# A graph network's build stage: its comparisons take their ramps from PSUM, and its products are evicted in halves from three PSUM regions

## The reference, cut to what matters

```python
x = _layernorm(x + _L0_gnn_ref(x, ..., src, dst, edge_type_3, node_type_3))   # typed messages, summed per node
x = _layernorm(x + _L1_gnn_ref(x, ..., edge_index, edge_weight))              # weighted sum of support[col] per row
x = _layernorm(x + _L2_gnn_ref(edge_index, x))                                # degree-normalised sum of neighbours
x = _layernorm(x + _L3_gnn_ref(x, edge_attr_64, src, dst, ...))               # sum of edge features @ W and h[src]
```

## Time and profile before

| | us |
|---|---|
| median of 3 runs (5166.46 to 5170.2) | 5168.8 |
| the profiled execution | 5166.42 |
| its span in the profile | 5164.6 |

### The profile page before, as it was taken

How to read it: one execution, slowest core, us unless ns; L and a number is a source line. 1 busy time by engine, 2 the same in 40 slices (tenths; PEclk the granted TensorE clock), 3 DMA queues, 4 the chain that set the end, 5 groups by cost and what they waited for, 6 DMA issues and landing times. The chain is left out here.

```text
span 5164.6 us, 99803 instructions
## 1 busy us (share of the span) xinstructions
PE 3645.9 (71%) x38930; PEld 2640.2 (51%) x38930; DVE 3255.0 (63%) x4527; ACT 1201.7 (23%) x2110; POOL 2201.7 (43%) x2050
## 2 busy tenths in 40 slices
PE   4457755555555555102888887399999599989997
PEld 3345655555555555102777776255555244444444
DVE  7886899999999999202777775766666500230022
ACT  0015655555555555100000000300000200010000
POOL 0051277777777777775777775000000003000300
PEclk9998899999999999656999999699999799989998
DMA  9646799999999999758878777288886367656664
GB/s 315 222 106 226 259 316 334 349 347 344 354 342 345 352 348 345 266 157 156 230 228 229 228 230 181 92 320 305 301 308 250 121 202 228 200 164 201 218 190 138
DMA packets 710790, 1297.10 MB, mean 251 GB/s; under 512 B 367384, under 2 KB 512428, under 8 KB 701260
## 3 DMA queue, kind: packets, MB, share of 16 engines
q1 hardware_dynamic: 579516, 823.86, 49.2%
q10 hardware_dynamic: 60300, 314.88, 15.5%
q0 software_dynamic: 70576, 152.66, 11.7%
HBM read 814.90 MB, written 529.03 MB: 260 GB/s over the span
## 5 line engine op out<-in xcount | busy, mean ns | idle before, releaser
L1394 POOL DMA_INDIRECT big<-typed_msgs,big x1216 | 1374.6, 1130 | 402.4 <-issue 365.7
L1439 PE MATMUL psum<-big 128*128 128x98 bf16 x7936 | 844.9, 206 | 607.3 <-DVE big L1421 567.7
L1439 PEld LDWEIGHTS psum<-big 128*128 128x128 bf16 x7936 | 761.3, 96 | 659.7 <-DVE big L1421 615.1
L2081 PE MATMUL psum<-big 128*128 128x512 bf16 (+1 forms) x4704 | 992.4, 374 | 82.5 <-DMA big<-adj 82.5
L1440 PE MATMUL psum<-big 128*128 128x49 bf16 x7936 | 831.4, 189 | 0.1
L1441 PE MATMUL psum<-big 128*128 128x49 bf16 x7936 | 829.0, 185 | 1.6 <-issue 1.6
L1441 PEld LDWEIGHTS psum<-big 128*128 128x128 bf16 x7936 | 782.0, 99 | 2.2 <-issue 2.1
L2081 PEld LDWEIGHTS psum<-big 128*128 128x128 bf16 x4704 | 460.4, 98 | 606.0 <-DMA big<-adj 83.0
L1440 PEld LDWEIGHTS psum<-big 128*128 128x128 bf16 x7936 | 765.6, 96 | 0.8 <-issue 0.7
L1666 PE MATMUL psum<-big 128*128 128x192 f32 x3648 | 643.8, 331 | 124.1 <-DMA big<-typed_msgs,big 105.1
L1891 PE MATMUL psum<-big 128*128 128x416 f32 x1984 | 656.4, 494 | 63.5 <-DVE big L1925 62.4
(11 more groups left out here) (318 smaller groups left out, 2799.0 us busy)
## 6 DMA issues: line engine op xcount, KB each, us to landing
wadj<-big ACTq DMA_DIRECT2D x248, 784.0 KB
big<-wadj SPq DMA_DIRECT2D x124, 1568.0 KB, 7.0
big<-adj SPq DMA_DIRECT2D x210, 896.0 KB, 4.8
big<-staged SPq DMA_DIRECT2D x304, 384.0 KB, 4.1
staged<-big SPq DMA_DIRECT2D x60, 1920.0 KB
adj<-big ACTq DMA_DIRECT2D x62, 1568.0 KB
big<-edge_feats SPq DMA_DIRECT2D x456, 128.0 KB, 4.2
edge_feats<-in_edge_attr SPq DMA_DIRECT2D x1, 51562.5 KB, 161.6
```

The costliest lines, as they stand in the source:

```text
L1394: pool.indirect_dma_start(out=sgot4[:, c, u, 0:D], out_offset=None, in_=typed_rows, in_offset=bass.IndirectOffsetOnAxis(ap=pairs4i[:, g, u ...
L1439: pe.matmul(to[:, 0:2 * NB], lo, hi_b[:, q, t, 0:2, 0:NB], start=True, stop=False)
L2081: last = pe.matmul(ps[c % 2][:, 0:len(blocks) * P], terms_[:, k, b * D:(b + 1) * D], ring_a[:, m % RA, 0:len(blocks), s * P:(s + 1) * P], ...
```

## The change

- Two groups of PSUM words, at the ends of banks 6 and 7, receive a copy of both ramps (89 words each). L1416 and L1418 read the ramp from there: blocks with even number from bank 6, with odd number from bank 7. The values compared with them and the three weight terms of L1421 stay in SBUF. (`term_words` is defined and not used.)
- The products go to three regions of two banks, each for eight nodes, where there were two regions of four banks for sixteen. PE counts `s_mm_b` per half batch and waits with half m until half m - 3 is evicted. DVE's and POOL's waits on `s_mm_b` are doubled in number and mean the same batches.
- ACT evicts each half by two copies of 8 x 49 = 392 elements; stores, loads and doubling stay where they were, after the second half. As the region is m mod 3, ACT's loop over the pairs of blocks is unrolled.

```diff
+        def made_in(q):
+            return psum[:, q * 1024:(q + 1) * 1024].rearrange("p (k x) -> p k x", k=2)[:, :, 0:4 * 2 * NB].rearrange("p k (t c) -> p k t c", c=2 * NB)
+        REGIONS, HALF = 3, TT // 2
+        def ramp_words(k):
+            return psum[:, (7 + k) * 512 - RAMP_WORDS:(7 + k) * 512]
+        def psum_ramps(k):
+            both = ramp_words(k).bitcast(BF16)
+            return both[:, 0:P], both[:, P:P + HC]
...
-                            at_least(pool, s_mm_b, i * (2 * BATCHES) + c * (2 * BATCHES) // SPER - BEHIND)
+                            at_least(pool, s_mm_b, 2 * (i * (2 * BATCHES) + c * (2 * BATCHES) // SPER - BEHIND))
...
+                for k in range(2):
+                    dve.tensor_copy(ramp_words(k), both_ramps).then_inc(s_clear, 1)
...
-                            dve.tensor_tensor(hi, in_twos(hi_ramp).to_broadcast([P, TT, HC // 2, 2]), all_columns(sbk, HC),
+                            dve.tensor_tensor(hi, in_twos(psum_ramps(k)[1]).to_broadcast([P, TT, HC // 2, 2]), all_columns(sbk, HC),
                                               ALU.is_equal).then_inc(s_hi_b, 1)
                             dve.tensor_tensor(lo_b[:, q, :, :].rearrange("p t (c d) -> p t c d", d=2),
-                                              in_twos(lo_ramp).to_broadcast([P, TT, P // 2, 2]), all_columns(sl, P), ALU.is_equal)
+                                              in_twos(psum_ramps(k)[0]).to_broadcast([P, TT, P // 2, 2]), all_columns(sl, P), ALU.is_equal)
...
-                        at_least(pe, s_adj_e, n - 1)
+                    at_least(pe, s_adj_e, m + 1 - REGIONS)
+                    for j in range(HALF):
+                        t = half * HALF + j
+                        to = made_in(m % REGIONS)[:, j // 4, j % 4, :]
...
+                            for half in range(2):
+                                m = 2 * (i * (2 * BATCHES) + k * BATCHES + b) + half
+                                act.wait_ge(s_mm_b, m + 1)
+                                made = made_in(m % REGIONS)
+                                t0 = b * TT + half * HALF
+                                act.copy(adj_st[:, k, :, t0:t0 + HALF].rearrange("p s (c t) -> p s c t", c=2),
+                                         made[:, :, :, 0:NB].rearrange("p c t s -> p s c t"))
+                                act.copy(wadj_st[:, k, b // 2, :, t0 % 32:t0 % 32 + HALF].rearrange("p s (c t) -> p s c t", c=2),
+                                         made[:, :, :, NB:2 * NB].rearrange("p c t s -> p s c t")).then_inc(s_adj_e, 1)
...
-                block_pairs(act, body)
+                for i in range(GB // 2):
+                    body(i)
```

More of the change, by code:

```diff
@@ L1239, in build @@
         hi_b = c.bitcast(BF16).rearrange("p (k t s c) -> p k t s c", k=2, s=4, c=HC)
-        c, at = cut(at, (P + HC + 1) // 2)
-        c = c.bitcast(BF16)
+        both_ramps, at = cut(at, (P + HC) // 2)
+        c = both_ramps.bitcast(BF16)
         lo_ramp, hi_ramp = c[:, 0:P], c[:, P:P + HC]
@@ L1348, in made_in, with term_words @@
         def made_in(q):
-            return psum[:, q * 2048:(q + 1) * 2048].rearrange("p (t c) -> p t c", c=P)
+            return psum[:, q * 1024:(q + 1) * 1024].rearrange("p (k x) -> p k x", k=2)[:, :, 0:4 * 2 * NB].rearrange("p k (t c) -> p k t c", c=2 * NB)
+        REGIONS, HALF = 3, TT // 2
+        RAMP_WORDS, TERM_WORDS = (P + HC) // 2, 3 * SLOTS
+        assert HC % 2 == 0 and RAMP_WORDS + TERM_WORDS <= 512
+        def ramp_words(k):
[3 more added lines that the diff above has]
+            return both[:, 0:P], both[:, P:P + HC]
+        def term_words(k):
+            return psum[:, (6 + k) * 512:(6 + k) * 512 + TERM_WORDS]
         with nc.Block() as block:
@@ L1404, in _ @@
                 dve.wait_ge(s_clear, 3)
+                for k in range(2):
+                    dve.tensor_copy(ramp_words(k), both_ramps).then_inc(s_clear, 1)
+                dve.wait_ge(s_clear, 5)
                 def body(i):
@@ L1428, in _, with half_batch @@
             def _(pe):
[L1429 to L1433, removed]
+                pe.wait_ge(s_clear, 5)
+                def half_batch(n, half):
+                    q, m = n % 2, 2 * n + half
+                    if half == 0:
                         pe.wait_ge(s_hot_b, n + 1)
-                        at_least(pe, s_adj_e, n - 1)
[L1436 to L1444, removed]
+                    at_least(pe, s_adj_e, m + 1 - REGIONS)
+                    for j in range(HALF):
+                        t = half * HALF + j
+                        to = made_in(m % REGIONS)[:, j // 4, j % 4, :]
+                        lo = lo_b[:, q, t, :]
+                        pe.matmul(to[:, 0:2 * NB], lo, hi_b[:, q, t, 0:2, 0:NB], start=True, stop=False)
+                        pe.matmul(to[:, NB:2 * NB], lo, hi_b[:, q, t, 2, 0:NB], start=False, stop=False)
+                        last = pe.matmul(to[:, NB:2 * NB], lo, hi_b[:, q, t, 3, 0:NB], start=False, stop=True)
+                    last.then_inc(s_mm_b, 1)
+                for n in range(NBATCH):
+                    for half in range(2):
+                        half_batch(n, half)
             @block.scalar
@@ L1456, in store @@
                     if b == 0:
-                        act.wait_ge(s_adj_e, i * (2 * BATCHES) + (k + 1) * BATCHES)
+                        act.wait_ge(s_adj_e, 2 * (i * (2 * BATCHES) + (k + 1) * BATCHES))
                     if b in WADJ_AT:
@@ L1582, in _ @@
                 dve.memset(psum[:, 0:Q * 512], 0.0).then_inc(s_clear, 1)
-                dve.wait_ge(s_clear, 5)
+                dve.wait_ge(s_clear, 7)
                 def one_hot(i, pos):
@@ L1645, in _ @@
             def _(pe):
-                pe.wait_ge(s_clear, 5)
+                pe.wait_ge(s_clear, 7)
                 def turn(i, own_):
```

2 lines of the change are left out of this document (1 added, 1 removed).

## The result

| | us |
|---|---|
| before, median of 14 runs (5160.61 to 5175.1) | 5168.45 |
| changed, median of 14 runs (5151.86 to 5161.56) | 5158.43 |
| ratio, with its 95% interval | 0.9981 (0.9973 to 0.9989) |
| the changed kernel's profiled execution, its span | 5155.02, 5153.2 |

The change gains 10 us of 5168, 0.19%. That is clear of the noise, since the interval of the ratio ends at 0.9989, and within the 0.2% that were called no change. In the changed kernel the gather of the staging is L1411, the two comparisons are L1436 and L1438, the product L1441, ACT's copies L1505 and L1507.

The account below looks back on a forecast made before the run. The prediction took POOL's row of gathers, locked in step with DVE's batches, to bound the build stage. 5166.4 + 0 (freed port) + 2 (comparisons) + 0 (halves, regions) = 5168 us; range 5140 to 5228.

Parts of the forecast that it names:

- the 0.2% that were called no change: Whole kernel: under 0.2% (10 us) a measurement can't tell from no change; chance of landing there 0.62.
- What bounds the stage: Build stage: POOL's row of gathers ends it; DVE, PE and ACT have 285 us of cover.
- Freed port, 0 us: Ramps from PSUM: comparisons stop delaying gathers, but the wait moves into the product, still two gathers per batch; 0 us.
- Rival (a): Gathers in the build: no lock, the comparison's 0.38 us per batch vanishes; -188 us, 4978 us; chance 0.07.
- The price of the comparisons, +2 us: DVE's two comparisons reading PSUM: -4 to +10 us over 496 batches, taken as +2.
- Rival (b): DVE's comparisons fall to the single pace, 1.50 us more per batch; +449 to +452 us, 5616 us; chance 0.12.
- The 65 ns more per instruction: DVE's PSUM reads: cycle table puts the fixed part 62 cycles above SBUF's, which would make the sum +64 us.
- Halves and three regions, 0 on the path: PE and ACT: split copies cost ACT 147 us, covered by its slack; 0 us, ends -27 and +51.
- rival (c): Thinner PE/ACT buffers: block-start waits reach DVE, over 30 us idle; +30 to +51 us, 5205 us; chance 0.11.
- The range's low end: Whole kernel: 5166 - 4 - 27, given as rounded up to 5140 us.
- The end of -218 us for the freed port: Ramps from PSUM, best case: 0.45 us of gather waiting freed per batch, 218 us in all.

Follow-up runs that it names:

- the mirror image: Changed kernel with ramps in SBUF, weight terms read from PSUM: 5936.7 us, ratio 1.0039 to the kernel before; with a third of the matmuls 5669.0 us, 0.959.
- halves_only: Changed kernel with both ramps read from SBUF again, halves and unrolled ACT code kept: 5926.0 us, ratio 1.0011 to the kernel before.
- third_after: Changed kernel with one of PE's three matmuls per node: 5669.8 us, ratio 0.957 to the kernel before.
- longer_batch: Changed kernel plus a DVE memset of 192 PSUM words per batch, ahead of the product: 5820.4 us, ratio 0.9837 to the kernel before; repeated 5822.8, 0.9852.
- third_longer: longer_batch with a third of the matmuls: 5635.7 us, ratio 0.952 to the kernel before, without one execution of 5939.6 us.

## Why the prediction came out as it did

**What bounds the stage: right.** POOL is all but alone from 2120 us on; without PE's matmuls the time is the same; and once no gather waits, the stage is 136 us shorter with DVE's end where it was.

**Freed port, 0 us: right, and by its mechanism.** Gathers of 0.94 and 1.38 us in turn were forecast and measured to 0.01 us, and two gathers start in 467 of the 468 batches in which DVE isn't held up. The same rule forecast the pattern of the mirror image and the wait in the longer batch; it did not forecast the gathers that wait near the memset. Rival (a), that the freed waits pay, is out. One of the rows behind it was miscounted: from 2423.36 to 3187.02 us not 100 but 145 gathers start inside an L1613. Of these 144 take 0.93 to 0.95 us, and the one of 1.48 starts in the last 6 ns of its L1613 and inside an L1588, so the reading stands.

**The price of the comparisons, +2 us: small as forecast, with the other sign.** They keep the double pace: 1212 ns for 2048 elements against 1215, 567 for 800 as before. Rival (b) is out, and with it the single rate that the Trainium skill gives in "VectorE: DVE Perf Modes", § The perf-mode tier table, for a tensor_tensor with a PSUM operand, at least for bf16 ramps of this form; the condition in the Trainium skill's "Vector Engine (DVE) Microarchitecture Reference", § 5.1, which names no memory, agrees. The 65 ns more per instruction, worked out in the prediction from the Trainium skill's cycle table, don't show either. The mean distance from start to start, over the undisturbed batches of the build, fell from 2.940 to 2.932 us, and 496 x 0.008 = 4 us is nearly all by which the last gather moved (4.6 us). That it comes of the ramps' place, and not of the halves or of the changed waits, the batches of halves_only and third_after show. The rows of the forecast gave -4 to +10 us; the value taken was at the wrong side of zero.

**Halves and three regions, 0 on the path: right, but ACT's cost was too low.** The copies take 500 and 564 ns, not 480 and 510, so ACT is busy 1055 us with them instead of 839, 216 more rather than 147. The fixed part was taken from a copy of another shape; the order in which a copy reads its region changed too, and the two aren't told apart. ACT's waits for the store of adj rose from 117 to 175 us, DVE's waits for PE from 10.5 us at 11 places to 28.9 at 21. With 2.8 us more of "issue" that is 31.7 us of idle time, at the mark of 30 that was set for rival (c), and DVE's last comparison starts 18 us later (2117.2 for 2099.6). POOL's last gather came 4.6 us earlier nevertheless, so POOL's sum took nothing of it, as argued, and the price of rival (c), 30 to 51 us, is out.

**The rest.** Forecast 5168, measured 5158. Of the 11.4 us between the two spans 6.4 are there when the next block's first gather starts (2404.4 and 2398.0): 4.6 at the last gather and nearly 2 in the seam. The other 5 arise later, in code that is the same. Runs of one kernel differ by 10 to 15 us, so these 5 are left unexplained. That the total fell within the 0.2% is therefore in part luck: the sum has no term for more than half of the 10 us. The range's low end was rounded the wrong way, since its terms give 5135 and not 5140; nothing hangs on it.

**The end of -218 us for the freed port was too far out.** It ignored that the transfers of the build stood at 0.98. Where all waits were gone, 142 us came.

## What to carry to other kernels

When one engine's short steps wait for another's long ones, follow the starts through one period before counting freed waits as gains: the two lock, and what counts is how many steps end in a period, a whole number. Removing part of the blocking only moves the wait; here the first half gave nothing, the other half alone only changed the pattern, and with both the waiting was gone and the time fell by what the next limit, probably the transfers, left of it. Count over a whole trace, too, and not only in one stretch: it was the count that showed the gathers near the memset, for which a rule read from a few rows did not hold. A version with both from PSUM and all its matmuls never ran where it could win, so its 142 us are shown only for the kernel without matmuls.

## What was unexpected of the hardware

- Among these three operations a gather waits only for one with two SBUF inputs, not for one that reads PSUM and SBUF: all 1216 took 938 to 957 ns once each of the three had one input in PSUM. That is as the Trainium skill has it in "SBUF — State Buffer", § Who interferes with whom.
- A memset of 192 PSUM words just ahead of the product changed that: 21 gathers of longer_batch and longer_batch_2 that started in it or just ahead of it, and 219 of third_longer that started 0.65 to 0.67 us ahead of the product, waited to the product's end. What the memset does to them is open.
- The gathers don't slow DVE: its batches last 2.940 us (ramps in SBUF) or 2.931 us (ramps in PSUM) with three gathers under way as with none.
- bf16 tensor_tensor with one PSUM input ran at 0.52 ns per element, (1212 - 567) / 1248, the pace of SBUF alone.
- The same kernel took 5167 to 5168 us on some chips and 5911 to 5922 us on three others. In halves_only, on one of these, the durations of DVE's operations and of undelayed gathers were nearly the same (1218 against 1216 ns for the 2048-element comparison, 0.94 us for a gather), but PE stood still 564 us for no reason in the profile. An extra 0.23 us per batch on DVE (2.931 to 3.165 us) made the whole 1.5 to 1.6% faster than the kernel before. Neither is explained.
- With the longer batch one execution went over from two gathers a batch to one, of 2.86 us, and was 300 us slower than its fellows.
